# Two attention helpers moved to earlier slots, and two PSUM banks exchanged, in a transformer block on one core

## What is computed

```python
q = heads((seq2 + b_self) @ Wq + bq)                  # 16 heads of 32
k = heads(concat(seq1 + b_prev, seq2 + b_self) @ Wk + bk)
v = heads(concat(seq1, seq2) @ Wv + bv)
score_prev = q @ k_seq1.T * SCALE, masked by seq_len1   # 512 keys
score_self = (q * k_seq2).sum(-1) * SCALE               # one own score a row
w = softmax(concat(score_prev, score_self))
attn = w[:, :-1] @ v_seq1 + w[:, -1:] * v_seq2
y = x + attn @ Wo + bo
out = y + concat(gelu(y @ W1 + b1) @ W2 + b2, gelu(..) @ We[expert] + be[expert])
```

## Time and profile before

| what | us |
|---|---|
| median of 3 runs | 1755.53 |
| lowest and highest | 1751.35, 1756.41 |
| the profiled execution | 1752.24 |
| its span (first to last instruction) | 1750.0 |
| TensorE busy | 1688.4 |
| VectorE, ScalarE, GpSimd busy | 861.4, 700.0, 662.2 |

### The profile page before, as it was taken

The page is one execution under the profiler, slowest core; times in us unless marked ns, Lnnn a source line. Parts: engine busy times, 40 slices in busy tenths (PEclk is TensorE's granted clock), DMA queues, the critical chain, the costliest instruction groups (busy, mean ns, idle before and its releaser), DMA issues.

```text
span 1750.0 us, 29595 instructions
## 1 busy us (share of the span) xinstructions
PE 1688.4 (96%) x9024; PEld 1289.4 (74%) x9024; DVE 861.4 (49%) x1370; ACT 700.0 (40%) x1223; POOL 662.2 (38%) x518
## 2 busy tenths in 40 slices
PE   5999999999999999999986999999999999999998
PEld 5766767667676676766744788888888888888886
DVE  4576675765757657577575433232323323232322
ACT  3354454544545445454454433233232323233321
POOL 3267594875948759577566001010000101010000
PEclk8999999999999999999988999999999999999999
DMA  6454544645446455463434423232231414132211
GB/s 139 85 123 100 117 116 90 138 99 114 110 95 135 98 115 110 99 133 93 110 104 129 146 66 75 65 55 73 45 86 45 87 48 86 54 61 79 37 25 24
DMA packets 392175, 157.90 MB, mean 90 GB/s; under 512 B 291666, under 2 KB 352082, under 8 KB 392098
## 3 DMA queue, kind: packets, MB, share of 16 engines
q1 hardware_dynamic: 360326, 144.00, 36.9%
q10 hardware_dynamic: 31772, 13.05, 2.9%
HBM read 77.75 MB, written 28.34 MB: 61 GB/s over the span
## 4 chain that ended last, share of the span: by engine, by line
PE 86%; DVE 6%; issue 4%; DMA 1%; SPq 1%; ACT 0%; DVEq 0%; POOL 0%; ACTq 0%
PE ps_proj L1382 17%; PE ps_max L1334 7%; PE ps_max L1335 7%; PE ps_max L1336 7%; PE ps_max L1423 7%; PE ps_num L1463 7%; PE ps_score L1450 6%; PE ps_proj L1404 5%; PE ps_num L1334 3%; PE ps_score L1334 3%; PE ps_score L1336 3%; PE ps_num L1335 3%; PE ps_score L1335 3%; PE ps_num L1336 3%; PE ps_max L1477 2%
## 5 line engine op out<-in xcount | busy, mean ns | idle before, releaser
L1034 DVE TENSOR_REDUCE m_col<-ps_max 128x1 f32<-128x512 f32 x512 | 333.6, 686 | 264.8 <-PE ps_max L1423 262.9
L809 ACT ACTIVATE p_f<-ps_score 128x512 f32<-128x512 f32 x512 | 303.3, 601 | 375.6 <-PE ps_score L1450 290.7
L674 POOL TENSOR_TENSOR p_sum<-p_sum,p_f 128x512 f32<-128x512 f32 x256 | 326.7, 1307 | 1.0 <-ACT p_f L809 1.0
L1237 DVE TENSOR_TENSOR h_lo<-h_f,h_hi 128x512 fp32r<-128x512 f32 x128 | 88.0, 688 | 409.8 <-ACT h_hi L915 409.7
L716 POOL TENSOR_TENSOR z_f<-z_f,a_raw 128x512 f32<-128x512 f32 x28 | 35.8, 1290 | 667.7 <-ACT z_f L924 646.4
L671 POOL TENSOR_TENSOR p_sum<-p_f 128x512 f32<-128x512 f32 x128 | 175.6, 1393 | 232.8 <-PE ps_max L1477 231.7
L1382 PE MATMUL ps_proj<-in_hi,w_hi 128*128 128x512 f32 x512 | 205.1, 401 | 14.4 <-POOL in_lo L679 7.2
L1450 PE MATMUL ps_score<-stacks 99*128 99x512 f32 x512 | 213.9, 419 | 4.6 <-ACT p_f L809 4.6
L1382 PE MATMUL ps_proj<-in_hi,w_lo 128*128 128x512 f32 x512 | 203.8, 398 | 0.0
L1382 PE MATMUL ps_proj<-in_lo,w_hi 128*128 128x512 f32 x512 | 203.5, 398 | 0.0
L1423 PE MATMUL ps_max<-stacks 97*128 97x512 f32 x512 | 182.8, 405 | 4.5 <-DVE m_col L1034 3.7
(11 more groups left out here) (141 smaller groups left out, 3013.6 us busy)
## 6 DMA issues: line engine op xcount, KB each, us to landing
stacks<-parts SPq DMA_DIRECT2D x384, 128.0 KB, 2.4
raw<-in_x_dram SPq DMA_DIRECT2D x128, 64.0 KB, 2.5
raw<-in_fside_BxSxS_dram SPq DMA_DIRECT2D x128, 64.0 KB, 2.7
spread<-own_scratch SPq DMA_DIRECT2D x128, 64.0 KB, 2.8
attn_scratch<-num SPq DMA_DIRECT2D x32, 256.0 KB, 3.0
x_raw<-in_x_dram SPq DMA_DIRECT2D x128, 64.0 KB, 2.2
we_raw<-in_L_cond_We_dram SPq DMA_DIRECT2D x32, 256.0 KB, 2.9
spread<-den_scratch ACTq DMA_DIRECT2D x124, 64.0 KB, 2.8
```

The source lines that it names most:

```text
L674: pool.tensor_tensor(p_sum[:, j], p_sum[:, j], p_f[:, i], ALU.add).then_inc(sum_made, 1)
L809: act.activation(p_f[:, i], ps_score[i % 2][:, :], ACT.Exp, scale=SCALE).then_inc(p_made, 1)
L1034: dve.tensor_reduce(m_col[:, n % C, n // C:n // C + 1], ps_max[n % 3][:, :], AX.X, ALU.max).then_inc(max_made, 1)
L1237: dve.tensor_tensor(h_lo[:, m % 2], h_f[:, :], f(h_hi[:, m % 2]), ALU.subtract).then_inc(h_lo_made, 1)
```

## The change

The numerator goes from slot 13 to slot 6 on VectorE. The denominators' matmuls go from slot 11 to slot 10 on TensorE, behind that slot's projections; the own scores and turned maxima stay in slot 11. On VectorE the denominator and the normalisation go from slot 12 to slot 11. The banks of denominators and own scores are exchanged, and each wait on a bank follows: the denominators need maximum tile 13 reduced, no longer 14, and the own scores tile 14, no longer 13. At the end of the attention the waits of the users of these two banks are exchanged in the same way.

```diff
-        ps_own = ps_max[1][:, 0:P]
-        ps_den = ps_max[2][:, 0:P]
+        ps_own = ps_max[2][:, 0:P]
+        ps_den = ps_max[1][:, 0:P]
...
-                        if i == 12 and started:
+                        if i == 6 and started:
+                            numerator(*after(b, g, -1))
+                        if i == 11 and started:
                             denominator(*after(b, g, -1))
                             if not (first and g < 2):
                                 normalize(*after(b, g, -2))
...
                         if i == 13 and started:
                             one_over_den(*after(b, g, -1))
-                            numerator(*after(b, g, -1))
...
                 if n == 1:
+                    wait(pe, den_made, G - 2)
+                if n == 2:
                     wait(pe, own_made, G)
-                if n == 2:
-                    wait(pe, den_made, G - 2)
...
-                pe.wait_ge(max_made, TILES * (G + 1) - 2)
+                pe.wait_ge(max_made, TILES * (G + 1) - 1)
...
                 if bound:
-                    pe.wait_ge(max_made, TILES * (G + 3) - 1)
+                    pe.wait_ge(max_made, TILES * (G + 3) - 2)
...
+                if c == 3:
+                    pe.wait_ge(den_made, C * B - 1)
                 out_project(0, c, first_o)
...
-                        if i == 11 and not (first and g == 0):
+                        if i == 10 and not (first and g == 0):
                             denominators(*after(b, g, -1), bound)
                         if i == 11 and bound:
                             own_scores(*nxt)
...
                     if m == 1:
-                        pe.wait_ge(den_made, C * B - 1)
+                        pe.wait_ge(own_made, C * B)
```

## The result

The changed kernel takes 1756.18 us (median of 22 runs, 1749.63 to 1759.83), the kernel before 1751.85 us beside it (22 runs, 1747.99 to 1756.41). The ratio is 1.0021, 95% interval 1.0013 to 1.0028, so 3.7 us slower by the ratio (4.3 by the two medians). Beside each other once more, in 12 and 29 runs, they took 1752.99 and 1752.20 us, ratio 0.9996 (0.9983 to 1.0009). The two intervals do not overlap. What is the same in every trace is the middle of the attention; what differs from run to run is its last batch and, nearly as much, all that comes behind it.

The account below looks back on a forecast made before the run. TensorE, busy 1688.4 of 1750.0 us, was taken as the bound. Terms - 7.2 - 0.8 + 8.7 - 0.5 = + 0.2 us, added to the 1755.53 median, gave 1755.7 us; 8-in-10 range 1749.5 to 1761.5.

Parts of the forecast that it names:

- Term 1: Attention's value run on TensorE no longer waits for the numerator: 7.2 us gained, 6.25 of it in six middle batches.
- Term 2: TensorE's small matmuls split into two blocks: 0.31 us lost in each of 28 groups, 8.7 us, bounds 0 and 11.
- own range from the bounds: Whole-kernel time range of 1751 to 1759 us that the prediction gave around its 1755.7 us.
- the part costed at nothing: Side effects on VectorE, GpSimd, banks and stores, taken as covered or unwaited for by TensorE in middle batches: 0 us.
- GpSimd's earlier sums: Sums starting about a slot earlier in three groups of four; no TensorE wait in middle batches, so worth nothing there.
- 0.8 and 0.5 us gained: 0.8 from the last batch's third group, where VectorE is late; 0.5 from earlier GpSimd sums at the seam of the halves.
- the free split (1): TensorE empties and fills behind other work, so splitting the small matmuls costs nothing: 1747.0 us; chance 0.11 for faster.
- the uncovered numerator (2): Numerator among VectorE's maxima delays TensorE: 1775 us with nothing covered, 1762 with a third; chance 0.08.
- late sums (3): GpSimd's sums come too late for slot 10's denominators, third group exposed: 7 us lost, 1763 us; chance 0.04.
- another holder of the value run (4): Something else, the last exponentials, holds the value run's start at 0.5 to 0.7 us: 1763.7 us; chance 0.02.

Follow-up runs that it names:

- num6_only: The kernel before with only the numerator moved from slot 13 to slot 6: 1747.09 us against 1754.49, ratio 0.9965.
- three_blocks: The changed kernel with the own scores moved ahead of slot 11's projections, giving three blocks of small matmuls a group: 1763.45 us, ratio 1.0060 to the kernel before.
- split_only: The changed kernel with the numerator put back in slot 13 and all else as changed: ratio 0.9987 to the kernel before.
- num6_again: A repeat, unedited, of the kernel before with only the numerator moved to slot 6: 1748.88 us, ratio 0.9966 to the kernel before.

## Why the prediction was right, and where its steps were off

The time was forecast within 0.3% of before, and it is: 1.0021 and 0.9996. The reason was two terms that cancel, and both are there. That the forecast of 1755.7 us lies so near the 1756.18 is luck in part: it starts from 1755.53, the median of three runs, and 22 runs of the same kernel have 1751.85. The forecast as a difference was + 0.2 us; measured were + 3.7 and, the second time, - 0.7 by the ratios (+ 4.3 and + 0.8 by the medians), and + 2.1 in the six middle batches. The "own range from the bounds", 1751 to 1759, does not follow from the bounds given (a split of 0 to 11 us alone reaches from 1747 to 1758); it is a judgement.

*Term 1.* Forecast 6.25 us for six batches, by the excess over 0.32 us. num6_only shows 660.11 - 654.20 = 5.9. Counting the distance between starts was right; the list of waits alone has 5.6 us for all groups, with 1.45 of it in the last batch.

*Term 2.* Forecast 0.31 us a group. Measured 662.22 - 654.20 = 8.02 us in 24 groups, 0.334 a group, of which 0.02 is the late copy (0.08 us in the third group of four). The size is right within a tenth. The sentence of the Trainium skill cited there ("TensorEngine Tiling (Array Packing)", Key Properties: a change of tiling mode drains TensorE) agrees with three_blocks, where each further block costs 0.31 us again; that a drain is what takes the time is not shown by any run.

*Together.* The forecast for the six middle batches was 24 x 0.31 - 6.25 = 1.2 us more; it was 2.1. The missing 0.9 is 0.6 of term 2 (8.02 against 7.44) and 0.3 of term 1.

*The step that was off, without moving the sum,* is in the part costed at nothing, on the earlier denominator, reciprocal and normalisation: "Nobody on TensorE waits for these in the middle batches, so they are worth nothing there"; and in adding the two terms as if each stood by itself. I had the numerator's own place as the only way out of the wait. split_only shows another: with the numerator left in slot 13, the six middle batches take 662.73 - 660.11 = 2.6 us more, and not the 7.4 us of 24 blocks, because the value run's wait shrinks from 1.04 to 0.08 us a batch. In the second and third groups the cover is the split's own surcharge, which makes TensorE late and leaves the numerator where it was; in the first and fourth it is that, the earlier numerator, or both. The sum was not moved, because a wait can be removed only once and the changed kernel removes it by slot 6. But what an item of the change is worth depends on the others: the split and what comes with it cost 8.0 us once the numerator is in slot 6 and 2.6 us where it is not; the numerator in slot 6 brings 5.9 us without the split and 0.5 us with it.

*Also wrong,* by less: GpSimd's earlier sums were taken for harmless in the middle batches. In the third group they lengthen VectorE's copy from 0.22 to 1.00 us, and TensorE waits 0.08 us for it.

*The last batch and the seam.* I took 0.8 and 0.5 us gained. No run bears out either: the last batch scatters from 121.2 to 126.9 us over 14 traces without regard to the numerator's place, and what follows it from 795.0 to 799.5. The prediction took the granted clock for one of three things that can move the end and then gave it no term; the 4.5 us by which the rest behind the last batch scatters, and which go with the clock, are twice what the change costs in the middle batches. The rivals: the free split (1) is refuted by num6_only and three_blocks, the uncovered numerator (2) by num6_only, late sums (3) and another holder of the value run (4) by the changed kernel's own trace.

*Open.* Why the first comparison gave 1.0021 and the second 0.9996 is not settled; a middle that costs 2.1 us lies between the two. The changed kernel's mean granted clock was 0.9834 in the first (22 runs, mean 1755.57 us) and 0.9846 in the second (12 runs, mean 1752.84 us). In both sets a run with 0.001 less clock is some 1.1 to 1.2 us longer, so the clock goes with about half of the 2.7 us between them; what makes it differ was not looked at. What decides whether the subtraction and the sums take turns was not tried.

## What to carry to other kernels

When TensorE is the bound, count what stands between kinds of matmuls as work: every separate block of 32-row matmuls costs here 0.31 us, with 8 of them or with 48, and a busy share hides it. Price each edit with the others in place: a wait also swallows what makes the waiting engine late, and two edits that remove the same wait don't add up. And when the whole scatters by more than the effect, compare stretches of the traces in which the granted clock is the same.

## What the runs showed of the hardware that was not expected

One subtraction on VectorE with both operands in SBUF lasts 0.68 us alone, up to 1.79 in turns with GpSimd's sums, and 5.46 to 7.27 us when it doesn't get its turn; in num6_again it ended at 893.94, 0.54 us behind GpSimd's last operation. This happened in 7 of the 10 traces of kernels with these subtractions in slots 0 to 3, and in one program it happened in one execution and not in the other. The Trainium skill, page "Advanced Engine Details and Errata", section Mode Summary, notes that VectorE's second SBUF port is shared with GpSimd, and that GpSimd's instructions and VectorE's in a two-port mode block each other. That the two engines hold each other up the traces show (0.68 against 1.79 and 7.27 us); whether these subtractions are in such a mode they do not. How long one operation can be kept out was the surprise: in num6_again over four sums and the own value of GpSimd, one behind the other.
